# The build stage of a graph kernel: the counts' second bf16 part made by a DVE subtraction, the row sums added up by POOL

## The reference

```python
h = relu(layernorm(x)); x = x + L0(h, edge_weight, src, dst, ...)   # weighted means over in- and out-edges, then gates
h = relu(layernorm(x)); x = x + L1(h, src, dst, edge_weight, alpha) # x, Ax, AAx, AAAx with weights
h = relu(layernorm(x)); x = x + L2(h, edge_index, ...)              # counts of edges, and linear attention
h = relu(layernorm(x)); x = x + L3(h, edge_index, edge_weight1, ...)# messages per edge, summed by dst
```

```python
wsum = jax.ops.segment_sum(w, src, num_segments=n)     # "row sums" of the weight matrix
deg = jax.ops.segment_sum(ones, col, num_segments=n)
```

## Time and profile before

| | |
|---|---|
| runs | 4103.9, 4106.24, 4116.88 us; median 4106.24 us |
| span of the profiled execution | 4131.5 us |
| the build stage in it | about 49 to 1126 us |
| busy: PE, DVE, ACT, POOL | 3483.2, 1463.3, 1265.5, 871.1 us |

### The profile page before, as it was taken

One profiled execution on the slowest core, in us unless ns is written; L12 is line 12 of the kernel. 1 busy time (PEld: TensorE's weight loads), 2 busy tenths in 40 slices (PEclk: granted clock), 3 DMA queues, 4 the chain that ended last, 5 costly groups with the idle time before them and its releaser, 6 DMA issues. The chain is left out here.

```text
span 4131.5 us, 85615 instructions
## 1 busy us (share of the span) xinstructions
PE 3483.2 (84%) x23502; PEld 2445.5 (59%) x23503; DVE 1463.3 (35%) x4278; ACT 1265.5 (31%) x4012; POOL 871.1 (21%) x928
## 2 busy tenths in 40 slices
PE   5888889999988888968999999997777677776777
PEld 2345556777744434435999999985444445444545
DVE  6766667777601200024431111132222222222223
ACT  5566667878701300014322211232000000000001
POOL 2000000000010000000000000024666566666663
PEclk8999999999999999997999999997777778787778
DMA  2011222333495589861432222341222222222222
GB/s 60 1 46 62 69 70 87 106 101 119 133 231 127 136 188 230 196 169 31 124 107 78 76 77 77 89 115 48 65 63 63 60 63 63 62 63 63 61 63 55
DMA packets 120056, 381.79 MB, mean 92 GB/s; under 512 B 33166, under 2 KB 74620, under 8 KB 106026
## 3 DMA queue, kind: packets, MB, share of 16 engines
q1 hardware_dynamic: 90958, 324.81, 29.5%
q0 software_dynamic: 25664, 51.90, 5.7%
q10 hardware_dynamic: 3154, 1.60, 0.2%
HBM read 294.59 MB, written 83.62 MB: 92 GB/s over the span
## 5 line engine op out<-in xcount | busy, mean ns | idle before, releaser
L2266 POOL DMA_INDIRECT edge_rows<-src_table,src_idx x784 | 776.6, 991 | 471.2 <-issue 193.4
L685 ACT ACTIVATE build_scaled<-build_lanes,w 128x128 f32<-128x128 bf16 x1132 | 428.6, 405 | 307.4 <-DVE build_lanes L640 275.0
L756 PE MATMUL build_ps<-build_keys,build_scaled 128*128 128x300 bf16 (+1 forms) x2264 | 492.2, 299 | 20.5 <-ACT build_scaled L685 17.8
L640 DVE TENSOR_SCALAR build_lanes<-key_id,lane,one_w 128x128 f32<-128x128 f16 x1132 | 389.1, 344 | 237.9 <-PE build_ps L756 181.9
L2410 ACT ACTIVATE edge_act<-edge_ps 128x512 f32<-128x512 f32 x196 | 116.9, 597 | 1147.6 <-remote 741.7
L2382 PEld LDWEIGHTS edge_ps<-edge_hot,edge_act 128*128 128x128 f32 x1760 | 297.8, 244 | 263.5 <-issue 261.5
L1108 PE MATMUL prop_ps<-prop_rows,y 125*128 125x500 f32 (+1 forms) x1050 | 408.3, 546 | 50.0 <-DMA prop_rows<-adj_rows 43.2
L2360 PE MATMUL edge_ps<-m_store,edge_hot_t 125*128 x2640 | 269.1, 249 | 205.0 <-issue 126.0
L748 PE MATMUL build_ps<-build_keys,build_lanes 128*128 128x300 bf16 (+1 forms) x1132 | 345.3, 305 | 87.8 <-DVE build_keys L642 65.4
L642 DVE TENSOR_SCALAR build_keys<-key_id,key,win_base 128x300 bf16<-128x300 f16 (+1 forms) x1132 | 406.0, 359 | 0.5 <-issue 0.2
L2382 PE MATMUL edge_ps<-edge_hot,edge_act 128*128 x1760 | 316.3, 332 | 94.8 <-issue 58.9
(11 more groups left out here) (368 smaller groups left out, 4762.4 us busy)
## 6 DMA issues: line engine op xcount, KB each, us to landing
prop_rows<-adj_rows SPq DMA_DIRECT2D x85, 1367.2 KB
cnt_panels<-build_cnt SPq DMA_DIRECT2D x50, 683.6 KB
adj_rows<-build_adj_t SPq DMA_DIRECT2D x25, 1367.2 KB
n<-cnt_panels SPq DMA_DIRECT2D x40, 683.6 KB
orders_panel<-cnt_panels SPq DMA_DIRECT2D x40, 683.6 KB
edge_dst_row<-dst_rows SPq DMA_DIRECT2D x196, 125.0 KB
h<-cnt_panels SPq DMA_DIRECT2D x20, 683.6 KB
prop_rows<-adj_rows SPq DMA_DIRECT2D x85, 158.7 KB
```

What stands on the lines that cost most here:

```text
L640: v.tensor_scalar(lanes[s][:], g.key_id[:, 0:128], g.lane[:, at], g.one_w3[:, at], ALU.is_equal, ALU.mult).then_inc(s_lanes[s], 1)
L685: a.activation(scaled[s][:], half(lanes[s], 1), ACT.Copy, scale=g.w12[:, bass.ds(t, 1)]).then_inc(s_scaled[s], 1)
L756: last = pe.matmul(ps[:, weight_bank(j), 0:KW[j % 2]], half(scaled[s], i), keys[s][:, 0:KW[j % 2]], start=False, stop=False, skip_group_ch ...
L2266: pool.indirect_dma_start(rows[s][:, i, :], None, dr.table, bass.IndirectOffsetOnAxis(ap=g.src_idx[:, t:t + 1], axis=0)).then_inc(s_rows[s ...
```

## The change

Four things change, all in `build_phase`. PE's `rest`, its semaphore and `minus` go. `low` moves from ACT to DVE: it waits for `s_high` and makes the second part in one TENSOR_TENSOR, PSUM minus the first part, to bf16; it stands after DVE's tiles of the window two later. DVE's `row_sums` go. POOL gets a program: it clears `by_lane` (125 x 25 x 125 f32) and, once all ten windows of a block have been copied out, adds the block's `adj` to it in one instruction of 3125 elements. DVE's last reduction then runs over the lanes of `by_lane`. The semaphore `s_sum`, for which ACT waits before it writes `adj` of the block after next, now comes from POOL.

```diff
-        rowsum = ph.sb("rowsum", [B, NB, NB])
-        minus = ph.sb("minus", [128, 128], BF16)
+        by_lane = ph.sb("by_lane", [B, NB, B])
...
         @block.vector
-            v.tensor_scalar(minus[:], g.ident[:], -1.0, None, ALU.mult).then_inc(s_minus, 1)
...
-            def row_sums(f, parity, i):
-
-                at = slice(5 * i, 5 * i + 5)
-                last = v.tensor_reduce(rowsum[:, bass.ds(f, 1), at].rearrange("p a k -> p (a k)"),
-                                       adj[parity][0:B, at, :], AX.X, ALU.add)
-                if i == 4:
-                    last.then_inc(s_sum, 1)
+            def low(w, j, parity):
+
+                v.wait_ge(s_high, w + 1)
+                v.tensor_tensor(in_block(cnt[parity][1], j), in_psum(count_bank(j, parity), j),
+                                in_block(cnt[parity][0], j), ALU.subtract).then_inc(s_low, 1)
...
                     spans.tiles(d, j, parity, one(j % 2, e))
+                    if j >= 2 or parity is not None:
+                        low(d * WPB + j - 2, *before(d, j, parity, 2)[:2])
                     if parity is not None:
                         if 1 <= j <= NG and j - 1 in MOVES[0]:
                             move(v, v.tensor_copy, d - 1, 1 - parity, pair, 0, j - 1)
-                        if j == SUM_AT[0]:
-                            v.wait_ge(s_weight, (d - 1) * WPB + WPB)
-                        if j in SUM_AT:
-                            row_sums(d - 1, 1 - parity, SUM_AT.index(j))
...
             v.wait_ge(s_sum, NB + 1)
-            v.tensor_reduce(g.wsum_src[:], rowsum[:].rearrange("p f h -> p h f"), AX.X, ALU.add)
+            v.tensor_reduce(g.wsum_src[:], by_lane[:], AX.X, ALU.add)
+
+        @block.gpsimd
+        def _(pool):
+            def block_of(d, parity, pair):
+                pool.wait_ge(s_weight, d * WPB + WPB)
+                pool.tensor_tensor(by_lane[:], by_lane[:], adj[parity or 0][0:B], ALU.add).then_inc(s_sum, 1)
+                pool.wait_ge(s_sum, d + 2)
+
+            pool.memset(by_lane[:], 0.0).then_inc(s_sum, 1)
+            pool.wait_ge(s_sum, 1)
+            blocks(pool, block_of)
...
         @block.scalar
-            def low(w, j, parity):
-
-                a.wait_ge(s_rest, w + 1)
-                a.activation(in_block(cnt[parity][1], j), in_psum(count_bank(j, parity), j), ACT.Copy).then_inc(s_low, 1)
...
         @block.tensor
-            def rest(w, j, parity):
-
-                pe.wait_ge(s_high, w + 1)
-                pe.matmul(in_psum(count_bank(j, parity), j), minus[:], in_block(cnt[parity][0], j), start=False, stop=True,
-                          skip_group_check=True).then_inc(s_rest, 1)
...
                     def after_first():
-                        if j >= 2 or parity is not None:
-                            rest(w - 2, *before(d, j, parity, 2)[:2])
```

More of the change, by code:

```diff
@@ L571, in build_phase @@
         s_high = ph.sem("high")
-        s_rest = ph.sem("rest")
         s_low = ph.sem("low")
@@ L581, in build_phase @@
         s_weights = ph.sem("weights")
-        s_minus = ph.sem("minus")
         s_tick = ph.sem("tick")
@@ L589, in build_phase @@
         N1_UP_TO = [0, 4, 7, 10, 13, 16, 19, 22, 25, 25]
-        SUM_AT = (2, 4, 6, 8, 9)
         PAIRS = 4
@@ L660, in block_of @@
                             move(v, v.tensor_copy, d - 1, 1 - parity, pair, 0, j - 1)
-                        if j == SUM_AT[0]:
-                            v.wait_ge(s_weight, (d - 1) * WPB + WPB)
-                        if j in SUM_AT:
-                            row_sums(d - 1, 1 - parity, SUM_AT.index(j))
-            v.sem_inc(s_sum, 1)
             blocks(v, block_of)
-            v.wait_ge(s_weight, NW)
-            for i in range(5):
-                row_sums(NB - 1, 0, i)
+            for j in (WPB - 2, WPB - 1):
+                low(NW - WPB + j, j, 0)
             for i in MOVES[0]:
@@ L721, in block_of @@
                         out_of_psum(w - 1, jb, pb, db if parity is not None else None, pair)
-                    if j >= 2 or parity is not None:
-                        low(w - 2, *before(d, j, parity, 2)[:2])
                     if parity is not None:
@@ L732, in _ @@
             out_of_psum(NW - 1, WPB - 1, 0, None, None)
-            for j in (WPB - 2, WPB - 1):
-                low(NW - WPB + j, j, 0)
             for i in MOVES[1]:
@@ L741, in _ @@
             counts = Counts(pe, g)
-            pe.wait_ge(s_minus, 1)
             def one(j, parity):
@@ L825, in _ @@
             pe.drain().then_inc(s_opened, 1)
-            for j in (WPB - 2, WPB - 1):
-                rest(NW - WPB + j, j, 0)
             for j in range(1, WPB):
```

## The result

The changed kernel takes 4226.2 us (median of 4 runs, 4223.63 to 4229.43), the kernel before 4105.07 us on the same occasion (4 runs, 4103.03 to 4116.88). The ratio is 1.0275, with a 95% interval from 1.0247 to 1.0304: 121 us slower, where 129 were forecast. The profiled execution of the changed kernel has a span of 4224.6 us.

A forecast was written before the change was run, and what follows sets the result against it. The build was taken as one ring, DVE to ACT to PE and back, with PE fullest. From 4106 us, -48 + 3 + 124 + 48 + 2 = +129 gave 4235 us, range 4155 to 4300.

The forecast's parts named there:

- The correction and ACT's copy (-48): In the build, dropping PE's 250 correction matmuls and ACT's second copy gains 48 us, bounds 20 to 76.
- `low` in, `row_sums` out (+3): On DVE in the build, subtractions replace reductions: +0.8 us a block, mostly covered, taken as +3 us, bounds 0 to 20.
- DVE's idle quarter: In the build DVE is busy 68 to 75 us of 100, so 20 us more work was thought covered.
- The hold is whole: At each POOL add, DVE's lanes or keys stand still until the instruction is over, all 6.8 us.
- the rival that POOL does not hold DVE: In the build, POOL's long add leaves DVE running, so work is only lost: -45 us, 4061 us; chance 0.08.
- the one that it lets it in by pieces: Beside POOL's add, lanes and keys slow to about half for some 10 us: +15 us, 4121 us; chance 0.09.
- What the holds cost (124): At 24 block turns PE resumes late: 15 turns at 5.75 us and 9 at 4.2 us, 124 us.
- the middle one: A middle block's turn, where PE resumes 5.7 us late; 15 of 24 turns were taken to be like it.
- The clock (48): Behind each turn's stall TensorE's clock falls to 0.50: 2.4 us in 14 turns, 1.4 in 10, 48 us.
- Rival 1: At the block turns DVE stops but TensorE's clock holds, so without the 48 us: 4187 us; chance 0.15.
- The ends (+2): At the build's start POOL's clearing costs 0 to 3.4 us, taken as +2; the last add and final reduction don't show.

The follow-up runs named there:

- `low` alone: Against the kernel before: correction matmul and ACT's second copy gone, DVE subtracts and keeps its reductions, POOL does nothing; 3815.12 us against 3860.33.
- the kernel with ten pieces: Against the changed kernel: each POOL add cut into ten of 250 or 375 elements, spread over the windows; 4087.9 us, the kernel before 4115.91.
- the filled kernel: Against the changed kernel: PE repeats group 0's transposes to eleven times in window 1 of every block; 4183.9 us, the kernel before 4115.91.
- The kernel with POOL alone: Against the kernel before: POOL adds the row sums, while PE and ACT keep the correction; 4015.64 us against 3860.33.

## Why the prediction was right, point by point

**The correction and ACT's copy (-48).** Right as far as the runs tell it. With the reductions kept and no POOL the build ends 48.5 us earlier, and PE's wait for ACT is 0.2 us. But that figure holds `low`'s cost on DVE too, and the reason given for 48, late windows full of matmuls, doesn't fit it: of the 48.5 us, 29.8 come in the first 10 blocks. So the nearness to 48 is in part luck. What is firm is the sum of this term and the next, -73 where -45 was forecast.

**`low` in, `row_sums` out (+3).** By this split of the -73 the one term with the wrong sign. `low` takes 463 and 490 ns, as read. The step that failed is that both lie "in DVE's idle quarter". DVE has idle time in the mean, but PE waited for keys for 65.4 us before the change already, 52 of them once the stage had begun, which the prediction passed over, and 107.5 with `low` alone. Taking the reductions off is worth 24.6 us, and PE's wait for keys falls by nearly as much, to 83.5. The gain of the change without its stops is 73 us, not 45.

**The hold is whole.** Right. Each of the 24 turns has one held record; the rival that POOL does not hold DVE, and the one that it lets it in by pieces, are out. An operation that reads PSUM is not held: the copy inside the last add took 0.68 us, and in the kernel with ten pieces one `low`, which reads PSUM and SBUF, took its usual 0.49 us inside a piece of 0.98 (at 859.34). The Trainium skill (SBUF — State Buffer, section "SBUF: two separate sides") says that of a POOL operation and a DVE operation in one of its two-port modes, whichever starts second is blocked until the other's instruction is over. The trace agrees on the length: the held records end 0.08 to 0.11 us after adds of 6.77 to 6.93 us. Which of the two started first it doesn't settle: in 8 of the 24 turns, the one shown among them, the held record begins 0.04 to 0.09 us before the add's. And that lanes and keys are in such a mode no run shows by itself.

**What the holds cost (124).** Mis-sized, some 141: 5.9 us a turn with the clock kept up, by the filled kernel, times 24. The step that failed is the 9 late turns with a lead of 3.1 to 4.5 us. That lead was read from a trace in which PE was slower and DVE had no `low` to make; the change shortens PE's way and gives DVE `low`, so nearly all turns look like the middle one that was costed at 5.75; which of the two counts more isn't told apart. The kernel with POOL alone still shows the larger lead, in late gaps of 3.5 to 5.0 us; the changed kernel's are 5.3 to 5.9 in all turns but one (2.53).

**The clock (48).** Right in kind, too large in size: 37 us over 24 turns. The early turns were right (13.4 us over 10, forecast 14), the late ones were not: 23.7 us over 14, 1.7 each where 2.4 were taken. The 2.4 came from one stall behind which the clock stayed low for 5.4 us (880.11); behind the late gaps of the changed kernel it is 4.3 in the mean, since a part of each low stretch lies inside the gap. By the medians' ratios it is 1.20% of 4116, or 49 us, but those carry some 12 us of uncertainty each, so the trace's figure is the one to use. Rival 1, the clock holds, was priced at 81 us over the kernel before; the kernel that makes it hold is 68 over it.

**The ends (+2).** The clearing does hold DVE, though it reads nothing: it ends at 51.52, the first lanes and keys at 51.60 and 51.68. PE's first matmul comes 1.47 us after the start of the first lanes, and 0.90 in the low-only kernel, which clears nothing: 0.6 us. At the other end the last add is over at 1222.64, before DVE's last move (1224.69), and the final reduction ends at 1228.29, before the next stage starts.

**The sum.** Measured on the build: -73 (with the clearing in it) + 141 + 37 = +105, and the traces say +106. Forecast: -48 + 3 + 124 + 48 + 2 = +129. The gain, with the ends, was 30 us larger than thought, the holds 17 costlier and the clock 11 cheaper: the terms' errors partly cancel, and the nearness of 4226 to 4235 is also owed to the 15 us of the medians that lie outside what the traces place. The interval of the forecast would have held either figure.

## What to carry to other kernels

A long POOL instruction beside a DVE stream that other engines wait for costs its length minus DVE's lead, once for every such instruction. Pieces shorter than the lead were not free either, but cost far less (1.5 us a block against 7.5). So ask how long one instruction is, and read the lead in the kernel as it will be after the change, not as it was. An idle share doesn't make an engine's time free: ask who waits for it, in the view of waits. Here PE's 52 us of waiting for keys before the change said that DVE's time was not free. And where a stall of TensorE can't be avoided, see what the clock does behind it.

## What the runs showed of the hardware that was not expected

- TensorE's granted clock fell to 0.50 at gaps of 1.94 to 2.72 us (26 of 33 with the add in two pieces), not only at those of over 4 us that the kernel before had the earlier trace rows; at gaps up to 1.62 us it did not begin to fall.
- The lost clock costs less than the stretch at half speed suggests: of 6.8 us only 4.2 in the mean lie behind the gap, and they cost 1.5 us a turn, not the 2.1 that half speed would cost a PE that never waits. That PE waits for DVE in a part of them anyway is the likely reason for the rest; no run tells it apart.
- Transposes that do nothing useful, 44 in a row from 1018.44, kept the clock at 1.00 at the turns, through holds of 6.8 us, and by the two ratios the kernel with them was 1.2% faster.
- A POOL memset that reads nothing held DVE's lanes and keys (1.34 and 1.15 us instead of 0.34 and 0.35), as an add does. With POOL alone it held DVE's making of `minus`: 1.97 us instead of 0.23.
- One instruction of 3125 elements takes 6.77 us and five of 625 take 5 x 1.53 = 7.66: cutting costs POOL 13% and gives the build 131 of the 179 us back.
